# One decoder layer on one core: normalised tokens a step earlier, two tiles per load, products stored by halves

## The reference

```python
x = x + attn(layernorm(x))          # 16 query heads of width 16, 4 key/value heads, biases, softmax, output @ Wo + bo
x = x + xattn(layernorm(x), ctx)    # 16 heads of width 64, keys and values from 77 context tokens, mask, @ Wo
x = x + ffn(layernorm(x))           # router over 8 experts, best 2, and one shared expert, each silu(x Wg) * (x Wu) Wd
```

## Time and profile before

| | |
|---|---|
| median of 3 runs | 1781.2 us |
| the profiled execution | 1781.99 us |
| its span | 1780.3 us |
| PE busy, of the span | 1694.7 us (95%) |
| DVE | 1386.3 us (78%) |
| ACT | 1112.4 us (62%) |
| POOL | 360.2 us (20%) |
| mean granted clock of PE | 0.979 |

### The profile page before, as it was taken

One profiled execution on the slowest core, in us unless ns is written; L12 is line 12 of the kernel. 1 busy time (PEld: TensorE's weight loads), 2 busy tenths in 40 slices (PEclk: granted clock), 3 DMA queues, 4 the chain that ended last, 5 costly groups with the idle time before them and its releaser, 6 DMA issues. The chain is left out here.

```text
span 1780.3 us, 36372 instructions
## 1 busy us (share of the span) xinstructions
PE 1694.7 (95%) x11950; PEld 1108.4 (62%) x11951; DVE 1386.3 (78%) x2651; ACT 1112.4 (62%) x2304; POOL 360.2 (20%) x431
## 2 busy tenths in 40 slices
PE   6899999999999999979889999997899999999998
PEld 3343333333333333356568999985798888888887
DVE  5699999999999999433678899984658666666663
ACT  4338888888888888912467888883226555544552
POOL 2100000000000000050043222221120455555540
PEclk9969999999999999999999999998999999999999
DMA  5702211111111220063211221114515233333335
GB/s 192 207 10 40 35 33 30 30 29 29 30 30 30 40 40 8 24 192 87 114 43 34 91 84 34 33 34 150 170 57 169 48 53 53 53 53 53 51 55 160
DMA packets 95823, 120.43 MB, mean 68 GB/s; under 512 B 18987, under 2 KB 76639, under 8 KB 94591
## 3 DMA queue, kind: packets, MB, share of 16 engines
q1 hardware_dynamic: 77936, 95.15, 19.3%
q0 software_dynamic: 13728, 18.88, 6.4%
q10 hardware_dynamic: 4047, 4.91, 0.9%
HBM read 71.25 MB, written 42.40 MB: 64 GB/s over the span
## 5 line engine op out<-in xcount | busy, mean ns | idle before, releaser
L506 DVE TENSOR_REDUCE half_max<-psA 128x1 f32<-128x512 f32 x1024 | 632.9, 683 | 9.9 <-PE psA L559 8.6
L538 ACT ACTIVATE PT<-psB 128x1024 f32<-128x1024 f32 x512 | 518.2, 1025 | 121.4 <-PE psB L569 121.2
L559 PE MATMUL psA<-KS,QS 48*128 48x512 f32 x1024 | 397.1, 466 | 4.1 <-PEq L104 2.0
L569 PE MATMUL psB<-QS,KS 50*128 50x512 f32 x1024 | 365.3, 454 | 0.2 <-ACT PT L538 0.2
L588 PE MATMUL psO<-PT,VG 128*32 128x256 f32 x4096 | 327.2, 392 | 4.5 <-ACT OU L528 0.4
L559 PEld LDWEIGHTS psA<-KS,QS 48*128 48x128 f32 x1024 | 162.8, 190 | 221.6 <-DVE half_max L506 162.6
L588 PEld LDWEIGHTS psO<-PT,VG 128*32 128x32 f32 x4096 | 82.0, 108 | 191.9 <-issue 114.2
L1741 PE MATMUL m_psY<-swd_high,m_hT 128*128 128x256 f32 x824 | 173.1, 293 | 12.7 <-DVE m_hT L1876 9.3
L1346 ACT ACTIVATE x_probs<-x_scores,x_neg_max 128x77 f32<-128x77 f32 x512 | 176.3, 358 | 3.4 <-DVE x_neg_max L1252 3.2
L569 PEld LDWEIGHTS psB<-QS,KS 50*128 50x128 f32 x1024 | 145.2, 186 | 13.1 <-ACT PT L538 10.5
L1741 PEld LDWEIGHTS m_psY<-swd_high,m_hT 128*128 128x128 f32 x824 | 134.2, 189 | 23.3 <-DVE m_hT L1876 12.4
(11 more groups left out here) (213 smaller groups left out, 2746.4 us busy)
## 6 DMA issues: line engine op xcount, KB each, us to landing
QS<-q_parts SPq DMA_DIRECT2D x96, 128.0 KB
q_parts<-part SPq DMA_DIRECT2D x16, 512.0 KB, 3.8
OT<-OU SPq DMA_DIRECT2D x32, 256.0 KB, 2.7
mx_kept<-cx_mx SPq DMA_DIRECT2D x4, 1232.0 KB, 10.1
cx_mx<-mx_kept SPq DMA_DIRECT2D x4, 1232.0 KB, 7.0
KS<-k_parts SPq DMA_DIRECT2D x32, 128.0 KB
xf_rows<-XF SPq DMA_DIRECT2D x32, 128.0 KB, 1.7
acc<-X SPq DMA_DIRECT2D x32, 128.0 KB, 1.8
```

What stands on the lines that cost most here:

```text
L506: dve.tensor_reduce(half_max[:, h * (TB // 2) + t % (TB // 2), n:n + 1], psA[:, bank_of(slot, 2 * v + r), :], axis=AX.X, op=ALU.max).then_ ...
L538: act.activation(PT[:, k % 4, 2 * a:2 * a + 2, :].rearrange("p h n -> p (h n)"), psB[:, u % 2, :, :].rearrange("p a n -> p (a n)"), ACT.Ex ...
L559: pe.matmul(psA[:, bank_of(slot, m), :], QS[top:top + KQ, slot, h // 2, t * P:(t + 1) * P], KS[top:top + KQ, slot, n * HALF:(n + 1) * HALF ...
L569: mm = pe.matmul(psB[:, u % 2, r, :], KS[top:top + KM, slot, c * P:(c + 1) * P], QS[top:top + KM, slot, a, half * HALF:(half + 1) * HALF], ...
```

## The change

Five things, in three phases:

- POOL fills all of KS with ones by one memset of 128 partitions; the counts that others wait for go down by one.
- DVE's order in a step of the projections becomes: statistics, mean and variance, `var_eps` of quad s; first and second low part of quad s-2; `xn` of quad s; third low part; copy of the values. So `xn` is made in the step of its statistics.
- OT has two places of two tiles; a load takes 256 columns (512 KB, runs of 1 KB), 16 loads in place of 32, the first four tiles loaded ahead of the phase. Load n waits until tile 2n-3 has been turned.
- The loops of SP and PE in the output projection are written out in place of hardware loops.
- The stores to `mx_kept` go by halves of the columns: four stores when 8 units are there, four when all 16 are. Eight stores make `mx_in` 128 (`MX_KEPT`), and later counts shift by that.

```diff
@@ phase_qkv, gpsimd @@
-            for n, top in enumerate((0, ROWS)):
-                pool.wait_ge(consts, 3 + n)
-                pool.memset(T["KS"].bitcast(F32)[top + 2 * HD:top + ROWS, :, :], 1.0).then_inc(consts, 1)
-            pool.wait_ge(consts, 5)
+            pool.memset(T["KS"].bitcast(F32)[:, :, :], 1.0).then_inc(consts, 1)
+            pool.wait_ge(consts, 4)
@@ phase_qkv, vector @@
             def step(quad):
-                if t := quad(1):
-                    i, e = t
-                    dve.wait_ge(rstd_done, at(i, 1, 1))
...
+                def take_low(n):
+                    if t := quad(2):
+                        i, e = t
+                        if isinstance(i, int) and i == 0 and n == 0:
+
+                            dve.wait_ge(w_loaded, 16 * 5)
+                            dve.wait_ge(va_set, 2)
+                        m, rows = MS[n]
+                        dve.wait_ge(high_done, at(i, NM, n + 1))
+                        dve.scalar_tensor_tensor(part[0:rows, e, 1, m, :], psQ[0:rows, m, :], bqk[0:rows, m:m + 1],
+                                                 part.bitcast(F32)[0:rows, e, 0, m, :], ALU.add, ALU.subtract).then_inc(low_done, 1)
+
...
+                take_low(0)
+                take_low(1)
+                if t := quad(0):
+                    i, e = t
+                    dve.wait_ge(rstd_done, at(i, 1, 1))
+                    if not peeled(i, 2):
+
+                        dve.wait_ge(tr_done, at(i, QUAD, -QUAD))
+                    for q in range(QUAD):
+                        dve.tensor_scalar(xn[:, e, q, :], X[:, i * QUAD + q, :], mean_var[:, e, q, 0:1], rstd[:, e, q:q + 1],
+                                          ALU.subtract, ALU.mult).then_inc(xn_done, 1)
+                take_low(2)
@@ load_rows @@
-def load_rows(eng, T, i, e):
-    eng.dma_start(T["OT"][:, e, :, :], T["OU"][:, :, bass.ds(i * P, P)]).then_inc(T["so_sums_in"][e], 16)
+def load_rows(eng, T, n):
+
+    eng.dma_start(T["OT"][:, n % 2, :, :], T["OU"][:, :, 2 * n * P:(2 * n + 2) * P]).then_inc(T["so_sums_in"][n % 2], 16)
@@ phase_self_out, sync @@
-            with sp.Fori(1, NT // 2) as j:
-                load(j * 2, 0)
-                load(j * 2 + 1, 1)
+            for n in range(2, NT // 2):
+                sp.wait_ge(rows_done, 2 * n - 2)
+                load_rows(sp, T, n)
@@ phase_self_out, tensor @@
-                    pe.wait_ge(sums_in[e], at(i - e, 8, 16))
+                    pe.wait_ge(sums_in[i // 2 % 2], 16 * (i // 4 + 1))
...
-            staggered(pe, NT, (0, 1, 2), step)
+            for n in range(NT + 2):
+                step(lambda lag, n=n: (n - lag, (n - lag) % 2) if 0 <= n - lag < NT else None)
@@ phase_context, sync @@
-            sp.wait_ge(low_in, UNITS)
-            for b in (2, 3):
-                for part in range(2):
-                    sp.dma_start(mx_kept[b, part, :, :, :], MA[:, b, part, :, :].bitcast(F32)).then_inc(mx_in, 16)
-            sp.wait_ge(mx_in, 64)
+            for half in range(2):
+                columns = slice(half * XH // 2 * SC, (half + 1) * XH // 2 * SC)
+                sp.wait_ge(low_in, UNITS // 2 * (half + 1))
+                for b in (2, 3):
+                    for part in range(2):
+                        sp.dma_start(mx_kept[b, part, :, :, columns], MA[:, b, part, :, columns].bitcast(F32)).then_inc(mx_in, 16)
+            sp.wait_ge(mx_in, MX_KEPT)
```

More of the change, by code:

```diff
@@ L174, in _ @@
                     if i == GROUP_AT[0]:
-                        sp.wait_ge(consts, 5)
+                        sp.wait_ge(consts, 4)
                     load_group(sp, T, GROUP_AT.index(i), GROUP_AT.index(i) % SLOTS)
@@ L216, in step @@
                         dve.bn_stats(stats[:, e, q, :], X[:, i * QUAD + q, :]).then_inc(stats_done, 1)
[L217 to L229, removed]
                     if not peeled(i, 2):
@@ L643, in self_out_places @@
     offset = T["place"]["QS"] + 4608
-    for name, shape in (("wo_sb", [P, KD, D]), ("bo_sb", [P, D]), ("OT", [P, 2, NKV, P])):
+    for name, shape in (("wo_sb", [P, KD, D]), ("bo_sb", [P, D]), ("OT", [P, 2, NKV, 2 * P])):
         T[name] = nc.alloc_sbuf_tensor_at(name, shape, F32, offset=offset)
@@ L656, in load_self_out @@
     eng.dma_start(T["bo_sb"][:, :], T["bo"].rearrange("(a n) -> a n", a=1).to_broadcast([P, D])).then_inc(T["so_w_in"], 16)
-    for e in range(2):
-        load_rows(eng, T, e, e)
+    for n in range(2):
+        load_rows(eng, T, n)
 def phase_self_out(nc, T):
@@ L691, in _ @@
         def _(sp):
-            def load(i, e):
-                sp.wait_ge(rows_done, at(i, 1, -1))
-                load_rows(sp, T, i, e)
-            with sp.Fori(1, NT // 2) as j:
-                load(j * 2, 0)
-                load(j * 2 + 1, 1)
+            for n in range(2, NT // 2):
+                sp.wait_ge(rows_done, 2 * n - 2)
+                load_rows(sp, T, n)
             for e in range(2):
-                sp.wait_ge(sums_in[e], 16 * (NT // 2))
+                sp.wait_ge(sums_in[e], 16 * (NT // 4))
         @block.gpsimd
@@ L735, in step @@
                     for g in range(NKV):
-                        mm = pe.transpose(psR[:, e, g * P:(g + 1) * P], OT[:, e, g, :], ident[:, :])
+                        mm = pe.transpose(psR[:, e, g * P:(g + 1) * P], OT[:, i // 2 % 2, g, i % 2 * P:(i % 2 + 1) * P], ident[:, :])
                     mm.then_inc(rows_done, 1)
-            staggered(pe, NT, (0, 1, 2), step)
+            for n in range(NT + 2):
+                step(lambda lag, n=n: (n - lag, (n - lag) % 2) if 0 <= n - lag < NT else None)
         @block.vector
@@ L792, in context_places @@
             assert offset >= T["context_from"] + 4 * B * KD * NPK * P
+MX_KEPT = 16 * 2 * 2 * 2
 CONTEXT_LOADS = 1 + 4 * KD
@@ L944, in _ @@
                 dve.tensor_copy(pair_columns(VT[:, :, u % KD, :], u // KD), pair_banks(u + UNITS)).then_inc(p_in[1], 1)
-            dve.wait_ge(mx_in, 64)
+            dve.wait_ge(mx_in, MX_KEPT)
             for n in range(1, BACK, 2):
@@ L965, in _ @@
                 act.activation(pair_columns(VT[:, :, u % KD, :], u // KD), pair_banks(u + UNITS), ACT.Copy).then_inc(p_in[0], 1)
-            act.wait_ge(mx_in, 64)
+            act.wait_ge(mx_in, MX_KEPT)
             for n in range(0, BACK, 2):
@@ L1072, in load_products @@
             def load_products(b):
-                sp.wait_ge(mx_in, 32 * b)
+                sp.wait_ge(mx_in, MX_KEPT + 32 * (b - 2))
                 for part in range(2):
@@ L1089, in _ @@
                     keep(i - L_XF)
-            sp.wait_ge(mx_in, 32 * B)
+            sp.wait_ge(mx_in, MX_KEPT + 64)
             sp.wait_ge(kept, 16 * 2 * NT)
@@ L1137, in scores @@
                         pe.wait_ge(xt_in, at(i, 1, 1))
-                        pe.wait_ge(mx_in, 32 * (i // TB) + 32)
+                        pe.wait_ge(mx_in, 32 * (i // TB) + MX_KEPT - 32)
                         for n in banks:
```

## The result

The changed kernel takes 1759.8 us (median of 4 runs, 1757.4 to 1760.7), the kernel before on the same chip 1783.4 (1780.0 to 1788.6): a ratio of 0.9863, 95% interval 0.9834 to 0.9892. The profiled execution took 1757.4 us. The forecast was 1757 us, in a range from 1752 to 1766. The total came out as forecast, 24.7 us less between the spans of the two profiles where the sum said 24.3; its terms did not.

| stage (us) | before | after | difference | forecast |
|---|---|---|---|---|
| projections | 79.8 | 72.9 | -6.9 | -11.4 |
| attention | 679.7 | 683.2 | +3.5 | 0 |
| output projection | 71.5 | 61.2 | -10.3 | -6.3 |
| context products | 59.7 | 50.6 | -9.1 | -6.6 |
| all that follows | 889.6 | 887.7 | -1.9 | 0 |

What follows compares the result with a forecast made beforehand. TensorE, busy 95% of the span, was taken as the bound, so only its stalls or low clock could give time back. Savings of 11.4 + 6.3 + 6.6 = 24.3 us from the 1781.2 us median gave 1757 us, range 1752 to 1766.

Steps and rivals of the forecast that it cites:

- Step of the projections: Projections: TensorE's wait for xn goes, so six steps take 6.6 us each, not 8.32, saving 10.3 us.
- C: Rival, projections: VectorE becomes the bound at 7.5 us a step, saving 4.9 not 10.3 us; total 1762; chance 0.09.
- SP's list still fits: Projections: SP's 2 us of stores and 5 to 6 us of group loads still fit the shorter steps.
- the -11.4: Projections: reordering and single fill together save 11.4 us, between 8 and 12.
- The fill: Projections' start: one memset instead of two takes 1.1 us off the chain to the first transposes.
- what one phase gains is carried to the end: Whole kernel: phases follow behind barriers, so one phase's gain or loss reaches the end; attention itself changes by 0.
- rival A: Attention: low clock lasts longer, each 10 us costing about 6; two groups more give 1805 us, slower; chance 0.04.
- Output projection: Two tiles per load remove 7.8 us of stalls, less 0.2 us per load for contested loads: -6.3 us.
- B: Rival, output projection: longer OT loads still collide, landing in 8.0 us; total 1780, no change; chance 0.07.
- Context products: Halved stores start ACT 5.7 us earlier and avoid low clock, about 2.5; less 0.6 for shorter runs: -6.6 us.
- the line through two sizes: Context products: 2.7 us fixed plus 2.54 us per MB, so half the stores take 8.9 us.
- D: Rival, context products: shorter runs move at half the rate, so the 6.6 us are lost; total 1763.5; chance 0.08.

Runs made afterwards that it cites:

- after_again: The changed kernel measured once more without any edit, beside three further kernels: 1761.6 us, ratio 0.9877 to the kernel before.
- group_split: Changed kernel with group 0's ten loads split, five behind quad 3's stores, five behind quad 4's; group 1's at attention's start: 1760.2 us, ratio 0.9864.
- first_only: Changed kernel with group 0's loads left behind quad 3's stores and only group 1's loads moved to attention's start: 1761.0 us, ratio 0.9837.
- only_proj: Kernel before with only the projections' part of the change (order on VectorE, single fill): 1779.5 us, ratio 0.9946.
- group_at_4: Changed kernel with group 0's loads behind quad 4's stores, not quad 3's, and group 1's at attention's start: 1759.3 us, ratio 0.9844.
- only_halves: Kernel before with only the mx_kept stores by halves: 1779.8 us, ratio 0.9966.

## Why the prediction was right, and where not

*Step of the projections: right.* `xn` is there in time and the period is 6.61 us, the 6.6 summed from starts. VectorE didn't become the bound (C).

*"SP's list still fits": the step that failed.* I had counted SP's issue times, 2 us of stores and 5 to 6 of loads. Even these are 7 to 8 us together, which fit into a step of 8.3 and not into one of 6.6. What counts is the landing, and the stores behind the loads land up to 11.2 us after their issue. They did so before as well, up to 10.1 us. SP and ACT of the kernel before, and between them the landing of the two stores (tile q_parts):

```profile
55.91 1.39 SPq L172 DMA_DIRECT2D q_parts<-part  x2
```

```profile
DMA to landing us min/median/max: 5.5/7.8/10.1
```

```profile
68.16 0.67 ACT L285 ACTIVATE part<-psQ,bqk_sb 64x512 fp32r<-64x512 f32 x1
```

The second of the two was issued at 56.8, so they were through by 66.9, and ACT came for them at 68.16, 11.4 us behind that issue: some 1.2 us of slack, in a row that was there to be read. After the change ACT asks at 56.9 (61.31 less 4.39), 6.9 us behind the issue at 50.0. Two steps of 6.6 us in place of 8.3 took 3.4 of these 4.5 us, the rest lies within the step, where TensorE no longer waits for `xn` ahead of ACT. With the landing 1.1 us later the slack became the wait of 4.4.

The cost is 72.9 less 68.3, 4.6 us, of which 1.7 is the low clock behind the wait (after_again, without it, began attention at 71.3); group_split shows that the -11.4 was to be had (79.8 to 68.3). That it is the place in the queue was shown by moving it, that two engines are late by the slices and packets above. Which transfer burdens these two is argued, not shown by a kernel of its own: of the 288 packets of 4 KB in first_only 62 start behind 51.5 us, and the two loads that write the keys in two copies (`to_broadcast([2, HD, S])`) have 64, 16 rows a copy. The Trainium skill (DMA: Bandwidth & Descriptors, "Why a DMA increments its semaphore by 16 and not by 1") says that a transfer is spread over the largest number of engines, up to 16, that divides the slowest dimension of both its sides; by that the keys' load would run on two, and the trace agrees with its 62 packets on two engines. No kernel here took it apart.

*The fill: -0.6, not -1.1.* The forecast took the 1.1 us of `var_eps` from an execution in which x had landed early. With one fill the chain waits for x. What is missing here the step ahead of the six gave: from first product to first product 8.14 us (12.79 to 20.93) in place of 8.72 (13.39 to 22.11).

*Attention: +3.5, not 0.* The prediction held that what one phase gains is carried to the end. Attention's clock is at 0.50 from 3 us behind its start at the latest, and it rose at 120.1 us in the profile before, at 121.7 after, at 121.5 in group_split: gains ahead of the rise are kept only in part if it doesn't come earlier too. This is rival A in small; its size was 0.41 us for each us of later rise behind the start (683.2 less 679.7, over 48.8 less 40.3 us from start to rise), about 4 us in ten where A had 6. A straight line through all 14 profiles has the same slope, and no attention phase lies more than 0.4 us off it, so the time from the start to the rise explains the length of the phase. What sets that time stays open. It was 40 to 79 us over the 14 profiles; in four that began attention between 71.3 and 72.9 (after, after_again, only_proj, group_at_4) it was 48.7 to 49.1, in first_only, which began at 72.6, 76.9. The Trainium skill (TensorE: Matmul & The Clock Gate, "Part 1: The HAM clock gate") says that the watch runs free of the kernel's start; no run here shows it, and it doesn't explain why the time was 48.7 to 49.1 us in four profiles and 76.9 in a fifth.

*Output projection: -10.3, not -6.3.* All stalls but 0.2 us went, where I kept 1.5 us for contested loads: the worst load landed in 4.9 us, just the time that it had, so B fell. (The five long intervals are 3.13 to 3.74 us, 7.7 over the pace, where the prediction read 3.3 to 3.8 and 7.8.) The pace of undisturbed tiles went from 1.87 to 1.83 us, 1.2 over 31 intervals, and the low clock at the phase's head, in the profile before and not in the one after, is the rest, some 1.7. That head stands in 5 of 14 profiles and comes and goes in kernels that are alike there; I count it as chance.

*Context products: -9.1, not -6.6.* Stores of half the columns landed in 3.3 to 9.0 us, as the line through two sizes had it (8.9), and neither D nor the 0.6 kept back for shorter runs came true. Without the low clock the gain is 4.0 us (54.6 to 50.6); the low clock behind the wait was 3.4 us where I put 2.5, and 1.7 is the low clock at the phase's head. That head stands in all six profiles without the whole change and in two of the eight with it, so chance or change is not shown. Behind the wait it varied too: 0, 1.7 or 3.4 us in five profiles with the old stores, none in nine with the new.

So the total was met by luck, by errors that cancel: 4.5 and 3.5 us lost that weren't foreseen, and 4.0, 2.5 and 1.9 won. The last is spread over phases whose work the change leaves alone; they took 886.9 to 892.5 us in the 14 profiles.

## What to carry to other kernels

When steps get shorter, ask of each transfer when it lands (the longest, not the median) and by how much that is early now; 1.2 us of slack were all that a faster step had here. To find what a wait belongs to, move its supposed cause and see whether the wait moves with it: here it went from one quad to the next with the group of loads, and was gone when the loads were cut in two behind different stores. Time won just ahead of a stretch at the low clock was worth some six tenths here, until the clock's rise has been seen to move as well.

## What the hardware showed that I had not expected

- A memset of 128 partitions of 4096 elements took 3.50 us, as long as one of 32.
- The clock stayed at its lower level until 40 to 79 us from attention's start with TensorE's row busy throughout (37.7 of 38.0 us from 82 to 120 in the profile before), and a second product beside each of the first pass's changed nothing that could be told from chance.
- Low stretches at the heads of phases cost about 1.7 us each, in the output projection (5 of 14 profiles) and in the context products (8 of 14, in only_halves twice as long).
- Two of the 16 DMA engines ended a run of loads and stores 5 us behind the others, at 25 GB/s each (first_only, 58.5 to 63.5 us).
